# A two-layer transformer block on one Trainium2 core: part of the causal mask moved from TensorE to VectorE, with a new order of all engines

## The reference

```
xn     = layernorm(x)
q,k,v  = xn @ qkv_w + qkv_b                 # 16 heads of 64
logits = (q . k) / 8 , masked causally with -0.7 * float32 max
x      = x + softmax(logits) @ v @ out_w + out_b + ffn(xn)   # silu gate, hidden 384
```

## Time and profile before

| what | us |
|---|---|
| median of 3 runs (lowest, highest) | 1507.27 (1505.23, 1508.43) |
| profiled execution, its own time | 1510.43 |
| its span, first to last instruction | 1508.7 |
| TensorE busy | 1456.1 (97%) |
| TensorE weight loads | 874.5 (58%) |
| VectorE busy | 1252.7 (83%) |
| ScalarE busy | 928.3 (62%) |
| POOL busy | 967.3 (64%) |
| mean granted TensorE clock, share of full | 0.99 |

### The profile page before, as it was taken

One profiled execution on the slowest core, in us unless ns is written; L12 is line 12 of the kernel. 1 busy time (PEld: TensorE's weight loads), 2 busy tenths in 40 slices (PEclk: granted clock), 3 DMA queues, 4 the chain that ended last, 5 costly groups with the idle time before them and its releaser, 6 DMA issues.

```text
span 1508.7 us, 26195 instructions
## 1 busy us (share of the span) xinstructions
PE 1456.1 (97%) x8770; PEld 874.5 (58%) x8770; DVE 1252.7 (83%) x1966; ACT 928.3 (62%) x1862; POOL 967.3 (64%) x752
## 2 busy tenths in 40 slices
PE   8899999999999999999999999887999999999998
PEld 6645545555455455555554555454677676776767
DVE  7577787788777888877788778377999999999997
ACT  4356666666666666666666666444766676657562
POOL 5134555546545556455456554519999999999895
PEclk9989999999999999999999999998999999999999
DMA  8058777777777777778777778400000000000000
GB/s 186 1 126 200 169 169 180 179 163 174 180 169 174 168 181 173 166 172 184 167 171 169 184 173 191 107 1 1 1 8 7 1 8 1 8 8 1 8 1 15
DMA packets 77136, 163.91 MB, mean 109 GB/s; under 512 B 31410, under 2 KB 43724, under 8 KB 77004
## 3 DMA queue, kind: packets, MB, share of 16 engines
q1 hardware_dynamic: 77004, 162.24, 46.6%
HBM read 9.08 MB, written 2.10 MB: 7 GB/s over the span
## 4 chain that ended last, share of the span: by engine, by line
PE 62%; SPq 13%; DVE 8%; DMA 5%; issue 5%; ACT 4%; POOL 2%; DVEq 0%; ACTq 0%; POOLq 0%
SPq L354 13%; PE accum L1083 11%; PE both L2772 10%; PE both L1022 6%; PE flips_all L2795 5%; DVE big L705 5%; DMA across<-big 5%; PE flips_all L2784 4%; PE flips_all L1022 3%; ACT big L528 3%; PE flips_all L2832 3%; PE misc L990 2%; PE accum L2784 2%; PE accum L2795 2%; PE flips_all L2818 2%
## 5 line engine op out<-in xcount | busy, mean ns | idle before, releaser
L447 POOL TENSOR_SCALAR big<-big,recip 128x1024 f32<-128x1024 f32 (+7 forms) x512 | 374.4, 745 | 447.0 <-DVE recip L697 446.8
L705 DVE STREAM_TRANSPOSE big<-big 128x896 f32<-128x896 f32 (+7 forms) x288 | 345.5, 1226 | 4.7 <-POOL big L447 2.6
L687 DVE TENSOR_REDUCE neg_max<-both 128x1 f32<-128x1024 f32 (+3 forms) x256 | 249.7, 1007 | 73.8 <-PE both L1024 73.8
L1083 PE MATMUL accum<-across,v_sb 128*64 128x256 f32 (+1 forms) x2560 | 278.5, 364 | 0.0
L528 ACT ACTIVATE big<-both,neg_max 128x1024 f32<-128x1024 f32 (+3 forms) x256 | 242.8, 951 | 44.6 <-DVE neg_max L687 44.5
L1083 PEld LDWEIGHTS accum<-across,v_sb 128*64 128x64 f32 x2560 | 169.0, 137 | 100.0 <-issue 25.8
L1022 PE MATMUL both<-qk_sb 64*128 64x512 f32 (+3 forms) x1024 | 215.8, 540 | 5.7 <-ACT big L528 3.5
L2772 PE MATMUL both<-slow_sb,h_T 128*128 128x512 f32 x384 | 182.5, 602 | 10.8 <-DVE xnT L2285 7.2
L1581 POOL TENSOR_TENSOR prod<-xnT,qs 128x1024 f32<-128x1024 f32 (+3 forms) x32 | 180.1, 5636 | 0.0
L1022 PEld LDWEIGHTS both<-qk_sb 64*128 64x128 f32 x1024 | 89.0, 187 | 118.8 <-issue 115.1
L528 ACT ACTIVATE big<-flips_all,neg_max 128x128 f32<-128x128 f32 (+3 forms) x256 | 131.7, 525 | 41.0 <-DMA across<-big 29.0
(11 more groups left out here) (223 smaller groups left out, 2381.2 us busy)
## 6 DMA issues: line engine op xcount, KB each, us to landing
across<-big SPq DMA_DIRECT2D x1024, 144.0 KB, 3.0
out<-x SPq DMA_DIRECT2D x8, 256.0 KB, 2.3
x<-in_L_attn_x SPq DMA_DIRECT2D x3, 512.0 KB, 5.7
slow_sb<-in_L_attn_w_slow SPq DMA_DIRECT2D x3, 512.0 KB, 7.7
w_qk<-in_L_attn_qkv_w SPq DMA_DIRECT2D x2, 512.0 KB, 6.4
xn<-in_L_ffn_W SPq DMA_DIRECT2D x1, 1024.0 KB
x<-in_L_attn_x SPq DMA_DIRECT2D x2, 256.0 KB, 2.9
qs<-in_L_attn_qkv_w SPq DMA_DIRECT2D x1, 512.0 KB, 6.1
```

The costliest lines, as they stand in the source:

```text
L447: pool.tensor_scalar(part, part, recip[:, u % 2, SLOTS.index(row), h:h + 1], 0.0, ALU.mult, ALU.add).then_inc(scaled, 1)
L687: dve.tensor_reduce(out=dst, in_=src, axis=AX.X, op=ALU.max, negate=True).then_inc(max_ready, 1)
L705: dve.transpose(part, part).then_inc(turned[group_of(row)], 1)
L1083: last = pe.matmul(dst, lhsT=values_of(u, j, h), rhs=keys_of(g, rows[n:n + 2], j, h), start=j == 0, stop=j == rows[n + 1])
```

## The change

The four low rows (steps 4, 5 and 6) get no mask product. VectorE adds the mask to the diagonal columns in PSUM itself, in one operation a step: 128x512 for rows 0 and 1 together, 128x256 for row 3 and for row 2 (two heads each). The maximum of such a step waits on a new semaphore for its own engine's addition. Rows 4 to 7 keep the product. SP's transfers are written as move(u - 1, ...) in the pass of u, and unit 31's go to the head of layer 1's list; VectorE's first maximum of a unit (row 7, head 1) moves to the end of the pass before.

```diff
+COVERED = (4, 5, 6)
@@ SP
             for u in range(UNITS):
                 if u == 2:
                     sp.wait_ge(xn_flipped, 2 * B)
                     sp.dma_start(w1_sb, W1.rearrange("x e h -> e x h")).then_inc(experts_loaded, 16)
                 if u == UNITS - 1:
                     for c in range(2):
                         for half in range(2):
                             k, use = use_of(u, "qk", c, half)
                             sp.wait_ge(bank_made[k], use)
                     sp.dma_start(w2_sb, W2.rearrange("x (j p) e -> p x j e", p=P)).then_inc(experts_loaded, 16)
                     sp.wait_ge(b2_cleared, 1)
                     sp.dma_start(b2_sb[0:X, :], b2).then_inc(experts_loaded, 16)
-                move(u, 0)
-                move(u, 1)
+                move(u - 1, 0)
+                move(u - 1, 1)
@@ VectorE
+            def cover(u, step):
+                if done(u):
+                    return
+                covers_at.meet(u, step)
+                scored(u, step, range(2))
+                rows = STEP_ROWS[step]
+                if len(rows) == 1:
+                    lo, hi = place_of(rows[0])
+                    part, wide = (both if step < SMALL else flips_all)[:, :, hi - P:hi], mask.unsqueeze(1)
+                else:
+                    part = flips_all[:].rearrange("p h (r k) -> p h r k", r=2)[:, :, :, 0:P]
+                    wide = mask.unsqueeze(1).unsqueeze(1)
+                dve.tensor_tensor(part, part, wide.broadcast_to(part.shape), ALU.add).then_inc(covered, 1)
@@ VectorE, maximum
+                scored(u, step, h or range(2))
+                if step in COVERED:
+                    dve.wait_ge(covered, covers_at(u, step))
@@ TensorE, place_scores
-                                  start=True, stop=z < hi)
+                                  start=True, stop=z < hi or step_of(row) in COVERED)
+                if step_of(row) in COVERED:
+                    return last
```

More of the change, by code:

```diff
@@ L205, in layer0 @@
                 ((0,), -1), ((4,), -1), ((1,), -1), ((6,), -1), ((2,), -1), ((5,), -1), ((3,), -1),
+            ])
+    covers_at = Tally([
+                ((4,), -1), ((6,), -1), ((5,), -1),
             ])
@@ L248, in layer0 @@
         qk_loaded, v_loaded, outw_loaded = sem("qk_loaded"), sem("v_loaded"), sem("outw_loaded")
[L249 removed]
+        covered, ident_made, mask_made, const_step, halves_made = sem("covered"), sem("ident_made"), sem("mask_made"), sem("const_step"), sem("halves_made")
         ints_scaled, setup_flipped, bq_scaled = sem("ints_scaled"), sem("setup_flipped"), sem("bq_scaled")
@@ L672, in keep_values, with scored @@
                                 ).then_inc(bank_kept[k], 1)
+            def scored(u, step, heads):
+                if step < SMALL:
+                    dve.wait_ge(scores_ready, scores_at(u, step))
+                else:
+                    for k in heads:
+                        dve.wait_ge(bank_made[k], uses_at[k](u, "s", step))
+            def cover(u, step):
[7 more added lines that the diff above has]
+                    part, wide = (both if step < SMALL else flips_all)[:, :, hi - P:hi], mask.unsqueeze(1)
+                else:
+                    part = flips_all[:].rearrange("p h (r k) -> p h r k", r=2)[:, :, :, 0:P]
+                    wide = mask.unsqueeze(1).unsqueeze(1)
+                dve.tensor_tensor(part, part, wide.broadcast_to(part.shape), ALU.add).then_inc(covered, 1)
             def maximum(u, row, *h):
@@ L734, in unit @@
                 maximum(u - 1, 7, 0)
-                maximum(u - 1, 7, 1)
+                cover(u - 1, 4)
+                maximum(u - 1, 1)
                 maximum(u - 1, 0)
-                maximum(u - 1, 1)
                 invert(u - 1, 0)
+                maximum(u - 1, 6, 1)
                 invert(u - 1, 4)
-                maximum(u - 1, 6, 1)
                 maximum(u - 1, 6, 0)
@@ L745, in unit @@
                     second_sums(u - 3, GROUPS[0])
+                cover(u - 1, 6)
+                turn(u - 1, 1)
+                maximum(u - 1, 2)
+                invert(u - 1, 1)
                 turn(u - 1, 7)
+                turn(u - 1, 6, 0)
                 turn(u - 1, 0)
[L748 to L751, removed]
                 turn(u - 1, 6, 1)
+                maximum(u - 1, 5, 0)
                 maximum(u - 1, 5, 1)
-                invert(u - 1, 6)
-                maximum(u - 1, 5, 0)
                 if u == 1:
@@ L759, in unit @@
                     second_sums(u - 3, GROUPS[1])
+                cover(u - 1, 5)
+                invert(u - 1, 6)
                 maximum(u - 1, 3)
@@ L763, in unit @@
                 invert(u - 1, 5)
+                maximum(u - 1, 4, 1)
                 maximum(u - 1, 4, 0)
-                maximum(u - 1, 4, 1)
                 if batch_over(u - 3):
@@ L771, in unit @@
                 turn(u - 1, 4)
+                maximum(u, 7, 1)
                 if batch_over(u - 3):
@@ L885, in _ @@
                 unit(u)
-            tails["vector"] = maximum, invert, turn, second_sums, second_variance
+            tails["vector"] = cover, maximum, invert, turn, second_sums, second_variance
         @block.tensor
@@ L1017, in place_scores @@
                 lo, hi = place_of(row)
+                last = [None, None]
                 for a in range(lo, hi, 512):
@@ L1021, in place_scores @@
                         part = slice(D * h, D * (h + 1))
-                        pe.matmul(scores_of(row, h)[:, a - lo:z - lo], lhsT=q[part, P * row:P * (row + 1)], rhs=k[part, a - lo:z - lo],
-                                  start=True, stop=z < hi)
+                        last[h] = pe.matmul(scores_of(row, h)[:, a - lo:z - lo], lhsT=q[part, P * row:P * (row + 1)], rhs=k[part, a - lo:z - lo],
+                                  start=True, stop=z < hi or step_of(row) in COVERED)
+                if step_of(row) in COVERED:
+                    return last
                 return [pe.matmul(scores_of(row, h)[:, P * row:P * (row + 1)], lhsT=ident_half[:], rhs=mask_half[:],
@@ L1167, in _ @@
             branch(2, (0,))
-            project(0, 1, 1)
+            pe.wait_ge(v_loaded, 16)
+            project_values(0, 1)
             hidden(3, 1, (0,))
@@ L1533, in _ @@
             last_move = tails["sync"]
+            last_move(UNITS - 1, 0)
+            last_move(UNITS - 1, 1)
             for t in range(ROWS):
```

97 lines of the change are left out of this document (48 added, 49 removed).

## The result

The changed kernel takes 1515.33 us, median of 13 runs (1510.91 to 1519.91), against 1507.27 for the kernel before, also 13 runs (1504.27 to 1511.50). The ratio is 1.0052 with a 95% interval of 1.0041 to 1.0063: 8 us slower. The profiled execution took 1516.75, its span is 1515.0; that is 6.3 us more than in the profile before. Three executions on record behind the ratios of the experiments (two of the kernel before, one of run 4) took 3.7 to 8.1 ms and are left out. M of a unit is, as in the prediction, the moment when VectorE has transposed the last of group 1.

The account below looks back on a forecast made before the run. The prediction took a loop through group 1's transfers as the bound, with TensorE nearly balanced. Its terms, -6.6 + 12.4 + 0.3 = +6.1 us on the profiled 1510.4, gave 1516.5, or 1513.4 for the median; range 1501 to 1521.

Parts of the forecast that it names:

- The bound: Attention units: one loop through group 1's transfers sets the 27.5 us pass, less than 0.5 us over TensorE's work.
- The rival of TensorE as the bound: Attention units: all four mask pairs count, 26.4 us off, 1493.4 with the stall of unit 31; chance 0.07.
- Removed products, 0.22 us a pass: TensorE: of four mask pairs dropped a unit only row 3's lies in the loop; 6.6 us saved over 30 passes.
- Additions at nothing: VectorE: three mask additions a unit, 1.5 us together, cost nothing; group 0's transfers keep 0.7 us of cover.
- The rival of group 0's loop: Attention units: additions use up the 0.7 us cover and group 0's transfers set the pace; 1520 to 1535; chance 0.11.
- Reordered: 0: Inside a unit: swapped heads and moved exponentials, copies and scalings cost 0, each still before the wait that ends last.
- the steady term: Attention passes: 0.22 us saved in each from row 3's mask pair, 6.6 us over 30 passes.
- The start, +0.3: Unit 0: no joins hide the moved projection and row 3's addition is exposed, against three pairs saved; +0.3 us.
- The stall of unit 31, +12.4: Last pass: unit 30's transfers queue behind SP's wait for unit 31's projections and the expert loads; +12.4 us.
- The second stretch of half clock (1.7): Unit 31: its 40 sums run at half clock after another idle stretch of TensorE, 1.7 us more.
- The rival with half clock in each unit: Attention units: TensorE's waits halve its clock each time, 51 us more, 1564; chance 0.07.
- The sum: Whole kernel: -6.6 + 12.4 + 0.3 = +6.1 us, a median of 1513.4.

Follow-up runs that it names:

- run 4: Changed kernel, but VectorE takes row 2's reciprocal between its two maxima of row 5, not behind the third addition: 1512.5 us, ratio 1.0029.
- run 6: Run 5's kernel, but all masks as products again and no additions on VectorE: 1504.6 us, ratio 0.9975 to the kernel before.
- run 7: Run 5's kernel plus two pairs of 128-column products a unit on TensorE, outside the loop: 1501.8 us, ratio 0.9953 to the kernel before.
- Run 8: Run 5's kernel with a second VectorE operation of the same size ahead of each addition: 1499.7 us, ratio 0.9943 to the kernel before.
- Run 3: Changed kernel, but POOL computes the batch statistics of units 10, 18 and 26 ahead of its scaling of row 2: 1508.9 us, ratio 1.0008.
- run 1: Changed kernel, but in the last pass SP issues unit 30's transfers ahead of its wait for unit 31's projections and the loads: 1503.4 us, ratio 0.9973.
- run 5: Changed kernel with the edits of run 1 and run 3 together: 1497.1 us, ratio 0.9929 to the kernel before.
- run 2: Kernel before with only the changed order of SP's list, TensorE's order as before: 1510.6 us, ratio 1.0011.
- run 9: Run 5's kernel, but ScalarE copies group 1's sums behind row 4's two exponentials, not ahead of them: 1498.5 us, ratio 0.9936 to the kernel before.

## Why the prediction was right, and where it was not

The forecast was 1513.4, a range of 1501 to 1521, and slower with 0.64. Measured 1515.3, slower. Point by point:

- **The bound.** A loop through group 1's transfers sets the pass, and TensorE's own work is close behind it. Runs 6, 7 and 8 show it: 0.88 us of products a unit are worth 7.4 us in all, not 26.4, and work added to TensorE or VectorE mostly vanishes. The rival of TensorE as the bound falls at its price of 26.4 us. How close the two bounds lie, the prediction saw only in the mean. In the 29 passes TensorE was busy 27.10 us of 27.46 before and did not wait at all in nine of them; in the changed kernel it was busy 26.29 of 27.35. Its idle time per pass went from 0.36 to 1.06 us, as forecast (0.4 to 1.1).
- **Removed products, 0.22 us a pass.** The row-3-to-row-4 part went from 7.67 to 7.45 us. Shown. The Trainium skill's figure for a product of 128 columns ("TensorE: Matmul & The Clock Gate", Back-to-back issue gap; by estimate 0.16 us a pair) is too low here: the measured 0.22 us holds.
- **Additions at nothing.** 0.69 and 0.42 us, group 0's transfers at M + 14.6, both as forecast; VectorE's wait on its own result was 0.13 us, not 0.3. Run 8 shows the cover. The rival of group 0's loop did not happen, though in a few passes the first exponential of row 7 was up to 1.2 us late (M + 2.4 in unit 2), which TensorE's waiting absorbed.
- **"Reordered: 0" was the step that failed.** The prediction moved POOL and VectorE's calls at no cost because each "still stands before the wait that ends last". In the plain units nothing speaks against it: from row 4's exponentials to M they took 5.0 us. In units 10, 18 and 26 POOL has 4.1 us more to do, and that work started 1.58 us later, of which 1.20 are row 2's reciprocal, put behind a maximum and the third addition (run 4). I had looked at a plain unit and never at the three with statistics. Run 3 prices it at 6.4 us: as much as the loop gained.
- **What offset it.** The plain passes gained more than 0.22 us each. From row 4's first exponential to M they took 5.0 us instead of 5.13, in some 5.5; row 2's first exponential, which waits for the landing, came 13.31 us after M on average for 13.27. Over 29 passes: -6.3 from the products, +1.9 from this last part with its three long ones in it, +1.1 up to row 2's exponential, -3.3 in all where the steady term was -6.6. Why the last part is 0.13 us shorter in a plain pass is not explained; about half of it lies in the reciprocal of row 4, which starts 1.69 us after that exponential (504.86) where it started 1.76 (507.98).
- **The start, +0.3, came out at -1.7.** I priced the projection and the addition, and missed that unit 0's copy of values no longer stands in front of the first exponential. In the kernel before, ScalarE waited for that copy and only then loaded its table:

```profile
67.26 0.60 ACT L516 ACTIVATE v_sb<-misc 128x512 f32<-128x512 f32 x1 [4.67 <-PE misc L1000]
67.88 1.28 ACT L528 ACT_TABLE_LOAD   x1
69.17 1.11 ACT L528 ACTIVATE big<-both,neg_max 128x1024 f32<-128x1024 f32 x1
```

  The changed kernel loads it while it waits for the maximum, and its first exponential comes 1.04 us earlier:

```profile
63.13 1.28 ACT L532 ACT_TABLE_LOAD   x1
68.13 1.11 ACT L532 ACTIVATE big<-both,neg_max 128x1024 f32<-128x1024 f32 x1 [3.71 <-DVE neg_max L709]
```

  Behind it a stretch of half clock fell away, which I had not looked for either. In the kernel before, TensorE waited 2.90 us for the exponentials of row 7, and the granted clock was 0.50 from 73 to 76 us:

```profile
71.61 2.21 PE L1022 MATMUL both<-qk_sb 64*128 64x512 f32 x8 [2.90 <-ACT big L528]
...
73.94 4.00 PE L961 MATMUL accum<-nrm_T,across 128*128 128x128 f32 x24
```

  In the changed kernel it waited 1.96 us and kept full clock:

```profile
70.56 1.77 PE L1048 MATMUL both<-qk_sb 64*128 64x512 f32 x8 [1.96 <-ACT big L532]
...
72.39 2.90 PE L986 MATMUL accum<-nrm_T,across 128*128 128x128 f32 x24
```

  How the 2.0 us between forecast and result divide between the two was not separated; run 7, where half clock comes at this place again, lost 1.2 us up to M of unit 2, its added products included.

- **The stall of unit 31, +12.4, came out at +12.2**, and run 1 prices it at 11.9 by itself. The steps inside it were less exact. Unit 30's group 0 started at M - 1.5, as forecast (M - 1.6), but landed 14.3 us after the first issue instead of 13.2, and the one stretch of half clock cost 2.1 us instead of 1.7. So unit 31's group 0 started at M + 28.3 instead of 26.7 and landed at M + 41.4 instead of 39.9. The second stretch of half clock (1.7) did not come: TensorE's wait before the 40 sums was 1.72 us and these ran at full clock. The errors cancel, and that is luck.
- **The clock.** In the middle of the attention TensorE waited up to 2.1 us (594.15) and never lost its clock: the granted clock is 1.00 from M of unit 2 to M of unit 31. The rival with half clock in each unit falls. The Trainium skill's case of a kernel throttled anew in each pass (the same page, HAM oscillation) is one that these waits did not bring about; no run here shows it.
- **The sum.** The two profiles differ by 6.3 us where +6.1 was forecast, and that is partly luck: the passes gained 3.3 us less than forecast (the statistics cost 6.4, a shorter end of the plain passes gave part of it back), and the start (2.0), layer 1 (0.9) and the stall (0.2) made up for it. The 1.9 us by which the median misses come from the offset of 3.1 us between profiled execution and median in the kernel before, which was 1.4 in the changed one.

## What to carry to other kernels

When a list is shifted by one pass against a fixed index (here the expert load at pass 31), ask of each special pass what now queues behind its wait: this cost 12 us of an edit whose body was right, and neither order alone did it. Follow a reordering through every kind of pass, the ones with extra work first, since a slack of 2 us in a plain pass can be gone there. And removing work from the busiest engine pays only until another bound is reached, here the loop of transfers: 7 of 28 us.

## What the runs showed of the hardware

TensorE kept full clock through waits of 1.72 us (before 960.0) and 2.06 us (from 594.15 in the changed kernel) and lost it after 2.69, 2.90 and 11.58. The length of a wait alone did not decide: behind the wait of 1.96 us at 68.6 the granted clock stayed at 1.00 in the changed kernel and in run 5 and fell to 0.50 in run 7, and in run 5 it stayed at 1.00 behind a wait of 2.66 us (before 998.5).

Unit 30's group 0, issued straight behind the two large loads, landed 14.2, 14.6, 14.2 and 13.5 us after its first issue (the changed kernel and runs 2, 4 and 3). Without the loads ahead it took 12.7 us in the kernel before and 13.1 to 13.9 in runs 1 and 5 to 9. So the loads may delay it by about 1 us; since single groups took up to 14.8 us with no load near (run 9), this is not shown.

An operation of VectorE that waits for the one just before it starts 0.13 us after its end (511.10 to 511.23), where independent ones start some 0.08 us before it.
